# Inverse roots by square root, reciprocal and a Newton step, and the ninth product to SBUF in every quarter but the last tile's

## The reference

```python
# x: (32, 64, 56, 56)
x = x + L0(_gn(x))      # group norm over pairs of channels; sign; 3x3 depthwise; prelu; bn; sign; 1x1; prelu; bn; + residual
x = x + L1(_gn(x))      # involution:
def L1(v, W, b):        # v: normalised x, C = 64, K = 3
    filters = einsum('bchw,oc->bohw', v, W) + b       # 9 filter planes per channel
    patches = the nine shifted copies of v (zero padded)
    return sum over the nine taps of patches * filters
def _gn(v): return (g - mean(g)) / sqrt(var(g) + 1e-5)  # g: two channels x 56 x 56
```

## Time and profile before

| | |
|---|---|
| median of 3 runs | 722.55 us (721.29 to 723.13) |
| span of the profiled execution, first to last instruction | 720.7 us; a time of its own beside the span is not recorded |
| busy: PE / DVE / ACT / POOL | 609.0 / 657.6 / 501.9 / 632.8 us (85% / 91% / 70% / 88%) |
| granted TensorE clock, mean | 0.987 |
| chain that ended last, largest shares | POOL 73%, issue 9%, DVE 8%, ACT 5% |

### The profile page before, as it was taken

The page is one execution under the profiler, slowest core; times in us unless marked ns, Lnnn a source line. Parts: engine busy times, 40 slices in busy tenths (PEclk is TensorE's granted clock), DMA queues, the critical chain, the costliest instruction groups (busy, mean ns, idle before and its releaser), DMA issues.

```text
span 720.7 us, 18683 instructions
## 1 busy us (share of the span) xinstructions
PE 609.0 (85%) x8017; PEld 258.6 (36%) x8017; DVE 657.6 (91%) x982; ACT 501.9 (70%) x629; POOL 632.8 (88%) x328
## 2 busy tenths in 40 slices
PE   2649789888888989898998988889888889898897
PEld 1314333333334334343433334333333434342233
DVE  4949889999999999999999999999999999999886
ACT  6967896968678596868869686877859686734110
POOL 2004589999999999999999999999999999999996
PEclk9979999999999999999999999999999999999999
DMA  5247596998999899898989899899989987897984
GB/s 204 84 137 126 109 263 146 208 226 186 255 194 253 186 224 231 163 259 186 265 184 244 194 192 241 186 259 189 252 184 208 225 187 166 190 204 166 200 173 136
DMA packets 34279, 142.10 MB, mean 197 GB/s; under 512 B 3348, under 2 KB 11540, under 8 KB 32276
## 3 DMA queue, kind: packets, MB, share of 16 engines
q0 software_dynamic: 17232, 75.87, 59.1%
q1 hardware_dynamic: 16940, 65.03, 25.4%
q10 hardware_dynamic: 24, 0.00, 0.0%
HBM read 26.03 MB, written 25.69 MB: 72 GB/s over the span
## 4 chain that ended last, share of the span: by engine, by line
POOL 73%; issue 9%; DVE 8%; ACT 5%; PE 2%; DMA 2%; SPq 0%; POOLq 0%; DVEq 0%; ACTq 0%
POOL prod L402 29%; POOL ob L426 13%; POOL prod L415 11%; POOL prod L408 9%; POOL prod L384 7%; DVE prod L939 4%; POOL st L371 2%; ACT unused L601 2%; POOL st L369 1%; PE tap_ps L541 1%; DVE xb L913 1%; DMA xb<-in_x_dram 1%; PE tap_ps L498 1%; ACT ab L601 1%; ACT q L601 1%
## 5 line engine op out<-in xcount | busy, mean ns | idle before, releaser
L939 DVE SCALAR_TENSOR_TENSOR prod<-tap_ps,bias,q 128x784 f32<-128x784 f32 x493 | 485.7, 1025 | 30.0 <-PE tap_ps L498 17.9
L498 PE MATMUL tap_ps<-q,w_t 64*64 64x392 f32 x2304 | 465.1, 502 | 52.1 <-DVE prod L939 26.3
L498 PE MATMUL tap_ps<-mirror,w_t 64*64 64x392 f32 x2304 | 459.9, 502 | 0.0
L498 PEld LDWEIGHTS tap_ps<-q,w_t 64*64 64x64 f32 x2304 | 153.8, 133 | 253.4 <-DVE prod L939 174.4
L402 POOL TENSOR_TENSOR prod<-prod 128x2352 f32<-128x2352 f32 x45 | 233.7, 5194 | 0.0
L601 ACT ACTIVATE ab<-tap_ps,col 128x784 bf16<-128x784 f32 x128 | 120.8, 995 | 50.9 <-PE tap_ps L541 50.3
L541 PE MATMUL tap_ps<-signs,dw_diag 64*64 64x392 bf16 x2304 | 133.1, 335 | 17.0 <-DVE prod L939 12.5
L498 PEld LDWEIGHTS tap_ps<-mirror,w_t 64*64 64x64 f32 x2304 | 139.3, 133 | 0.2 <-issue 0.2
L426 POOL TENSOR_TENSOR ob<-prod 128x784 f32<-128x784 f32 x63 | 132.3, 2100 | 4.5
L541 PEld LDWEIGHTS tap_ps<-signs,dw_diag 64*64 64x64 bf16 x2304 | 70.2, 108 | 105.4 <-issue 54.5
L415 POOL TENSOR_TENSOR prod<-prod 128x784 f32<-128x784 f32 x45 | 104.2, 2315 | 0.0
(11 more groups left out here) (118 smaller groups left out, 335.0 us busy)
## 6 DMA issues: line engine op xcount, KB each, us to landing
prod<-prod POOLq DMA_DIRECT2D x63, 1176.0 KB, 10.2
out_dram<-ob SPq DMA_DIRECT2D x31, 784.0 KB, 5.9
xb<-in_x_dram SPq DMA_DIRECT2D x15, 1568.0 KB, 12.4
mirror<-q SPq DMA_DIRECT2D x64, 203.0 KB, 4.5
xb<-in_x_dram SPq DMA_DIRECT2D x2, 784.0 KB, 5.6
out_dram<-ob SPq DMA_DIRECT2D x2, 392.0 KB, 2.3
prod<-in_L_conv_W_dram SPq DMA_DIRECT2D x1, 288.0 KB
prod<-in_L_conv_pw_weight_dram SPq DMA_DIRECT2D x1, 32.0 KB
```

The costliest lines, as they stand in the source:

```text
L498: mm = pe.matmul(rows3(tap_ps[to, slot, side, 0:CH]), w_t[own, k, :], moving, start=True, stop=True)
L939: v.scalar_tensor_tensor(place.rearrange("p j (a b) -> p j a b", b=WD), psum.rearrange("p j (a b) -> p j a b", b=WD), s_(t, B4) if k == 4 ...
```

## The change

GpSimd no longer makes the inverse roots. ScalarE forms the variance in two steps and its square root (`root`, three instructions in a chain), VectorE takes the reciprocal (`invert0`, `invert1`), and ScalarE corrects it by one Newton step (`inverse_root`, four instructions in a chain; the last writes the inverse root). The scaling copies of the old result go. VectorE's reciprocal of the second norm's scale goes as well: `B4` is now variance times inverse root, made on ScalarE.

`POOLED` gains quarter 0: in tiles 0 to 14 all four quarters are pooled, and `pair` and `add_early` stay only in quarter 2 of the last tile. The schedule tables are rewritten, and five delays move: on GpSimd the order in a cycle of nine units becomes `add_wide`, `add35`, fold, `final`.

```diff
-            def rstd(t, shuf, own, other, var, var_done, power, pow_done):
-                wait(pool, shuf, t.count(1, 1))
-                pool.tensor_scalar(s_(t, var), s_(t, own), s_(t, other), EPS * N_GROUP, ALU.add, ALU.add).then_inc(var_done, 1)
-                wait(pool, var_done, t.count(1, 1))
-                pool.tensor_tensor(s_(t, power), s_(t, var), minus_half[:, 0:1], ALU.pow).then_inc(pow_done, 1)
...
+            def root(t, shuf, own, other, part, var, root_, step, done):
+                act.wait_ge(shuf, t.count(1, 1))
+                acts(s_(t, part), s_(t, other), ACT.Copy, scale=1.0 / N_GROUP, bias=EPS).then_inc(step, 1)
+                act.wait_ge(step, t.count(2, 1))
+                acts(s_(t, var), s_(t, own), ACT.Identity, scale=1.0 / N_GROUP, bias=s_(t, part)).then_inc(step, 1)
+                act.wait_ge(step, t.count(2, 2))
+                acts(s_(t, root_), s_(t, var), ACT.Sqrt).then_inc(done, 1)
+            def inverse_root(t, inv_done, var, inv, fix, out, fix_step):
+                act.wait_ge(inv_done, t.count(1, 1))
+                acts(s_(t, fix), s_(t, var), ACT.Identity, scale=s_(t, inv)).then_inc(fix_step, 1)
+                act.wait_ge(fix_step, t.count(3, 1))
+                acts(s_(t, fix), s_(t, fix), ACT.Identity, scale=s_(t, inv)).then_inc(fix_step, 1)
+                act.wait_ge(fix_step, t.count(3, 2))
+                acts(s_(t, fix), s_(t, fix), ACT.Copy, scale=-0.5, bias=1.5).then_inc(fix_step, 1)
+                act.wait_ge(fix_step, t.count(3, 3))
+                return acts(s_(t, out), s_(t, fix), ACT.Identity, scale=s_(t, inv))
...
-                v.reciprocal(s_(t, INV1), s_(t, QS)).then_inc(inverse_done, 1)
+            def invert0(t):
+                dve.wait_ge(root0_done, t.count(1, 1))
+                v.reciprocal(s_(t, INV0), s_(t, ROOT0)).then_inc(inv0_done, 1)
+            def invert1(t):
+                dve.wait_ge(root1_done, t.count(1, 1))
+                v.reciprocal(s_(t, INV1), s_(t, ROOT1)).then_inc(inv1_done, 1)
...
 -    'load': -115,
+    'load': -102,
...
- 'sum1': -16,
- 'mean1': -15,
- 'square1': -12,
- 'var1': -11,
- 'rstd1': -8,
- 'q0': -11,
- 'q1': -3,
+    'sum1': -19,
+    'mean1': -18,
+    'square1': -12,
+    'var1': -12,
+    'root1': -11,
+    'invert1': -11,
+    'q0': -11,
+    'q1': -2,
...
-FOLD_DELAY = 4
-EARLY_ADD_DELAY = 14
+FOLD_DELAY = 6
+EARLY_ADD_DELAY = 8
 MEAN_DELAY = 12
-WIDE_ADD_DELAY = 21
-LATE_ADD_DELAY = 22
-POOLED = 1, 2, 3
+WIDE_ADD_DELAY = 19
+LATE_ADD_DELAY = 23
+POOLED = 0, 1, 2, 3
...
-TAKE_DELAY = 13
+TAKE_DELAY = 15
...
-OUT_DELAY = 23
+OUT_DELAY = 25
```

More of the change, by code:

```diff
@@ L767, in _ @@
                     signs_second(30, H)
-                for t in tiles("inverse", g, 1):
+                for t in tiles("b4", g):
                     centre_bias(t)
@@ L987, in _ @@
                             what(t)
-                for place, what in (("mean0", mean0), ("var0", var0), ("mean1", mean1), ("var1", var1),
-                                    ("inverse", centre_bias), ("inv_z", inv_z), ("ratio", ratio)):
+                for place, what in (("mean0", mean0), ("var0", var0), ("invert0", invert0), ("mean1", mean1), ("var1", var1),
+                                    ("invert1", invert1), ("inv_z", inv_z), ("ratio", ratio)):
                     for t in tiles(place, g):
@@ L996 @@
 COURSE = {
-    'load': -115,
- 'sum0': -74,
- 'mean0': -72,
- 'sign0': -69,
- 'square0': -66,
- 'var0': -63,
- 'rstd0': -65,
- 'scales0': -61,
- 'inv_z': -56,
- 'ratio': -54,
- 'job0': -56,
- 'job1': -45,
- 'job2': -33,
- 'job3': -26,
- 'sum1': -16,
- 'mean1': -15,
- 'square1': -12,
- 'var1': -11,
- 'rstd1': -8,
- 'q0': -11,
- 'q1': -3,
- 'inverse': -8,
+    'load': -102,
+    'sum0': -72,
+    'mean0': -71,
+    'sign0': -69,
+    'square0': -66,
+    'var0': -63,
+    'root0': -62,
+    'invert0': -61,
@@ L1042 @@
- 1: {'sum0': -100,
-     'mean0': -100,
-     'sign0': -84,
-     'square0': -82,
-     'var0': -82,
-     'rstd0': -82,
-     'scales0': -75,
-     'inv_z': -36,
-     'ratio': -36,
-     'job0': -39,
-     'job1': -29,
-     'job2': -24,
-     'job3': -18,
-     'sum1': -10,
-     'mean1': -10,
-     'square1': -9,
-     'var1': -9,
-     'rstd1': -8,
-     'q0': -8,
-     'q1': -7,
-     'inverse': -6},
- 2: {'sum0': -62,
-     'mean0': -59,
-     'sign0': -58,
-     'square0': -53,
-     'var0': -49,
-     'rstd0': -51,
-     'scales0': -46,
-     'inv_z': -46,
-     'ratio': -44,
-     'job0': -42,
-     'job1': -37,
-     'job2': -32,
-     'job3': -27},
+    0: {
+        'sum0': -71,
+        'mean0': -105,
+        'sign0': -68,
+        'square0': -68,
+        'var0': -66,
+        'root0': -62,
+        'invert0': -66,
+        'scales0': -62,
+        'inv_z': -60,
+        'ratio': -60,
+        'job0': -65,
+        'job1': -64,
+        'job2': -59,
+        'job3': -58,
+        'sum1': -48,
+        'mean1': -48,
+        'square1': -47,
+        'var1': -46,
+        'root1': -45,
+        'invert1': -45,
+        'q0': -43,
+        'q1': -43,
+        'b4': -40},
@@ new lines @@
+    1: {
+        'sum0': -100,
+        'mean0': -99,
+        'sign0': -86,
+        'square0': -82,
+        'var0': -82,
+        'root0': -82,
+        'invert0': -81,
+        'scales0': -75,
+        'inv_z': -36,
+        'ratio': -36,
+        'job0': -39,
+        'job1': -29,
+        'job2': -24,
+        'job3': -18,
+        'sum1': -9,
+        'mean1': -10,
+        'square1': -9,
+        'var1': -9,
+        'root1': -8,
+        'invert1': -8,
+        'q0': -8,
+        'q1': -8,
+        'b4': -3},
@@ L1076 @@
+    2: {
+        'sum0': -62,
+        'mean0': -59,
+        'sign0': -58,
+        'square0': -53,
+        'var0': -49,
+        'root0': -48,
+        'invert0': -47,
+        'scales0': -47,
+        'inv_z': -46,
+        'ratio': -43,
+        'job0': -40,
+        'job1': -37,
+        'job2': -32,
+        'job3': -27},
 }
 PROLOGUE = {
-    'bias': -49,
- 'turn_w': -43,
- 'copy_w': -45,
- 'signs_rest': -43,
- 'square_0': -58,
- 'square_1': -53,
- 'square_2': -52,
- 'square_3': -47,
+    'bias': -52,
@@ L1087 @@
+    'turn_w': -41,
+    'copy_w': -45,
+    'signs_rest': -43,
+    'square_0': -58,
+    'square_1': -54,
+    'square_2': -52,
+    'square_3': -47,
 }
```

83 lines of the change are left out of this document (31 added, 52 removed).

## The result

The changed kernel takes 736.8 us (median of 4 runs, 735.9 to 738.1) beside 722.84 for the kernel before: a ratio of 1.0195, 95% interval 1.0178 to 1.0211. It is slower by 1.95%, where 717.6 us and a gain of 0.7% were forecast, and it lies outside the range of 711 to 729. The profiled execution's span is 734.0 us against 720.7.

What follows compares the result with a forecast made beforehand. GpSimd and VectorE were taken to hold each other at 41.28 us a tile. The span 720.7 - 7.3 (tiles) + 1.3 (folds) + 1.0 (start) = 715.7, plus 1.85 to the median, gave 717.6 us; range 711 to 729.

Steps and rivals of the forecast that it cites:

- The folds' landing: GpSimd's wide adds: folds get 12.8 to 13.3 us to land; late ones lose 0.1 per tile, +1.3 us.
- Folds that land after 13.1: Late fold DMAs, named within the first rival as giving the same result, 723 us or so.
- the first rival: VectorE's waits in order behind ScalarE cost 1.5 per tile and use up the gain: 723 us or so; chance 0.23.
- a wide add released by a DMA: Sign of being wrong, on GpSimd: `add_wide` idle before it, released by a DMA; no size given.
- 13 tiles: Steady part: GpSimd's tile at 40.72 instead of 41.28, -7.3 us over 13 tiles, before the folds' 0.1 per tile.
- The pooled quarter: GpSimd's steady tile: a pooled quarter takes 10.18 us, near the late 10.12 rather than 10.46; four make 40.72.
- Start: First tiles: longer root chain, +1.2 twice, against GpSimd not blocked and one VectorE pair less; +1.0 us taken.
- Last two tiles: End: the last tile keeps its kinds of quarters; no term in the sum; an uncovered early add would cost 1.8.
- Waits for `final` grown to 1 or more per tile: Sign of being right: VectorE's waits for GpSimd's `final` grow from 0.69 to 1 or more per tile.
- The second: Rival on GpSimd: pooled quarter stays at 10.46, tile grows by 0.56, +8.3 us, 731 us; chance 0.10.
- The third: Rival on ScalarE: `Sqrt` changes tables in each tile, 43 per tile, about 746 us; chance 0.08.

Runs made afterwards that it cites:

- h: The changed kernel with the load of x issued 13 units earlier, at its place before the change: 751.07 us, ratio 1.0391.
- q: The changed kernel with the load of x waiting for one more quarter's `final`: 719.94 us, ratio 0.9969 to the kernel before.
- b: The changed kernel with loads of x for tiles 3 to 15 bringing 98 of 3136 columns only: 719.9 us, ratio 0.9955.
- j: The changed kernel with `FOLD_DELAY` 4 instead of 6, so folds are issued two units earlier: 727.47 us, ratio 1.0065.
- n: The kernel of i with the load of x a quarter later (-93): 766.34 us, ratio 1.0596 to the kernel before.
- e: The kernel before with quarter 0 pooled too, inverse roots still on GpSimd: 751.23 us, ratio 1.0385.
- a: The changed kernel with the five delays of GpSimd's steps as before: 726.59 us, ratio 1.0054.
- i: The kernel of d plus a square root ahead of the first tile and that tile's reciprocal and ratios behind the second tile's sum: 713.01 us, ratio 0.9867.
- d: The changed kernel with the old five delays and `POOLED = 1, 2, 3`, the roots' removal alone: 715.91 us, ratio 0.9901.
- r: The changed kernel with q's wait, `FOLD_DELAY = 4`, `EARLY_ADD_DELAY = 14` and i's two first-tile edits: 721.44 us, ratio 0.9989.
- k: The changed kernel with mirrors moving one row in place of 7 from the fourth tile on: 721.92 us, ratio 0.9987.

## Why the prediction was wrong

The step that failed is **"The folds' landing"**. The term was 0.1 a tile, +1.3 us; it measured 14.1 us, in 11 tiles. The room was nearly right (12.7, from the fold at 308.28 to its wide add at 320.97, where 12.8 to 13.3 were forecast). The landing was not: the 13.1 of the kernel before was carried over to a queue whose order the same diff changed, and the fold behind the burst landed after 14.0 to 15.5 in the tiles with a load. At 13.1 it would have been late by 0.4; at 14.5 it is late by 1.8, and its quarter takes 11.96 instead of 10.1. The forecast saw that 13.1 stood at the edge of the new room; it gave no allowance for a landing that moves. The load's move as such isn't what failed, for h takes it back and loses 14 us more; the loss comes from the cut of the room from 17.5 to 12.7, with a load that still stands in the burst. GpSimd's account closes with the folds: 522.4 us busy, 14.1 of waits and 5.8 between the sums make the 542.3; q has 522.0, 0.4 and 6.1, and takes 528.5. "Folds that land after 13.1" stood inside the first rival, for 723 us, and a wide add released by a DMA among the signs of being wrong: the right mechanism with too small a price.

Term by term against the span of 715.7 forecast and 734.0 measured:

- *13 tiles*: forecast 13 x (40.72 + 0.1) = 530.66, measured 542.34: +11.68. The pooled quarter itself was right, and better than 10.18: 10.1, tiles of 40.4 in b and q, where 40.72 was forecast.
- *Start*: forecast +1.0, measured +3.85: +2.85. The chain was costed for the second root only, and there rightly: from the square's end to q 2.1 before, 3.35 after, +1.25 for the +1.2 forecast. The first tile's first root was taken as hidden, as GpSimd's had been, but ScalarE does it in order ahead of `relu_act`, in 4.4 us instead of 0.95, and these hold a second table load of 1.28 that the sum didn't have. The first product comes 5.6 us later (53.1 against 47.6); why 3.85 of these are left at the cut, no run shows.
- *Last two tiles*: forecast 0, measured +3.80. The fifteenth pays for its fourth pooled quarter with no load or root to gain from, and the last for the fold's place (25.1 us in j).

11.68 + 2.85 + 3.80 = 18.3, the whole difference.

**VectorE.** "Waits for `final` grown to 1 or more per tile" was wrong: none. VectorE is relieved by 0.4 a tile (39.07 busy against 39.50; forecast 38.7), but its first products wait for mirrors that land with a fold. n shows that path alone. In the changed kernel it hardly reaches GpSimd, which sets the tile: 1.6 us of waits for VectorE in all, beside 14.1 for folds. Both hang on the folds, and no run took one away and left the other, so how the 1.3 a tile (41.7 against 40.4) would divide is not measured.

**Rivals.** The first rival's own waits, VectorE's shuffles for ScalarE, were 0.3 a tile where it set 1.5. The second (10.46 a quarter) falls by e, and by a, whose common tiles take 40.7 in the old order. The third falls: two table loads in the whole run, none in the steady part. The Trainium skill (ScalarE: Activation LUTs, Table sets: the hidden batching unit) has sqrt anchor a set of its own; the runs agree, for the changed kernel's second load stands at its first square root (22.78), and go further. In i, where a square root comes first, one load serves the whole run, so that set holds sign and square too.

**The larger error** is behind all of this: even with every fold in time no version with the fourth pooled quarter reached the roots alone (b, q and r, 719.9 to 721.4 us, against d's 715.9). The forecast compared GpSimd's new tile, 40.7, with the old tile, 41.28, and not with what the roots' removal gives by itself, 40.18 (d). The pooled quarter moved the beat from VectorE back to GpSimd for nothing. The best version, i, keeps three pooled quarters and mends a part of the start (124.6 us to the cut, 128.5 in d, 119.3 before): 713.0 us, 0.9867 of the kernel before (0.9855 to 0.988).

What stays open: by what rule the DMA engines pass from one queue to the other (the last section has what the packets show), and what starts the single tiles of 42 to 43 us in a and r, which have no wait for a fold and TensorE's clock at 0.50 for a stretch.

## What to carry to other kernels

When a diff moves DMAs in their queue's order, take the landing times of the others as unknown: list what will leave beside what, and compare each landing with its room to the tenth, before and after: a late landing that an old order hid shows once its room is cut. Cost a change of two parts part by part, each against what the other alone gives, not against the kernel before. And look at what a unit number really orders: a step moved past no other instruction of its queue hasn't moved, and one moved past a single DMA can cost 50 us.

## What the runs showed of the hardware

**Small DMAs behind a large one.** The first mirror of a tile, issued 1.2 to 7 us behind a fold, landed within about 1.4 us of the fold's landing, whether it moved 203 or 29 KB; with 29 KB all mirrors took 7.0 us in the median. The packets say why. In k a fold leaves at 296.05 and two mirrors of 29 KB at 299.64 and 300.28. From 298 to 304 us, and then from 304 to 305.5, the queues of GpSimd (q0) and SyncE (q1) move:

```profile
q0 software_dynamic: 236, 1.11, 106.7%
```

```profile
q1 hardware_dynamic: 288, 0.06, 21.2%
q0 software_dynamic: 20, 0.02, 8.1%
```

In the first stretch SyncE's queue has no packet: the mirrors wait until nearly all of the fold's packets are through. From 127 to 664 us 77 of the 6144 packets of small mirrors in k, and 12 of 6656 in the changed kernel, start within the middle 90% of a fold's packets, which cover 57 to 58% of the time; in the kernel before it is 800 of 6656. The Trainium skill (DMA: Bandwidth & Descriptors, Queues, rings and completion order) says that a DMA engine serves its queues in turn and drains a whole packet of one, typically some 9 to 17 descriptors, before it switches. A fold has 256 data packets in the trace, 16 for each of 16 engines if they are spread evenly (an estimate); if those are the descriptors of one packet in the skill's sense, its rule gives what is seen, and no run here shows whether they are.

**TensorE's clock.** TensorE's wait ahead of the first products is followed by slower matmuls. Stretches of 2 us in the changed kernel, busy times as above, then the granted clock:

```profile
308.50:310.50 2.00, 0.86 (x8) 0.57 (x12) 1.46 (x3) 2.00 (x1) 2.00 (x2) 0.82 0.37 69
310.50:312.50 2.00, 2.00 (x17) 1.01 (x14) 1.03 (x1) 1.62 (x3) 2.00 (x2) 0.50 0.96 169
312.50:314.50 2.00, 2.00 (x29) 1.15 (x25) 1.99 (x4) 0.81 (x2) 2.00 (x1) 0.83 1.09 195
```

TensorE was busy 0.86 of 2.00 us, waiting for mirrors, and then ran at 0.50, the level of 1.2 GHz: 17 matmuls began in those 2 us, 29 in the next. From 50 to 700 us the granted clock falls below 0.95 at 10 places after, 2 before, 3 in d and 2 in i. What this costs a tile was not measured.
